# Cross-attention mask of a decoder layer: four slices of 32 keys against a small identity, in place of a 63-row product in two passes

## The chip, the cores and the metric

One core of one Trainium2 chip runs the whole kernel. The metric is the device time of one execution in microseconds (us); a median over several runs is compared. Line numbers (L290) are those of the kernel before.

## The reference, cut to what matters

The program is one pre-norm decoder layer over 32 batches of 128 rows by 128 features, all in f32: self-attention with 16 heads of 8, then cross-attention with 16 heads of 64, then a mixture of 8 experts (one per row, picked by an argmax) with a shared expert. The change is in the cross-attention:

```python
def xattn(q, k, v, wq, wk, wv, wo):
    qh, kh = rope(q @ wq.T), rope(k @ wk.T)            # 16 heads of 64
    scores = einsum('bhqd,bhkd->bhqk', qh, kh) * 64 ** -0.5
    i, j = arange(128)[:, None], arange(128)[None, :]
    scores = where((j <= i) & (j >= i - 32), scores, -1e30)
    out = einsum('bhqk,bhkd->bhqd', softmax(scores), v @ wv.T)
    return out @ wo.T
```

So a query sees its own key and the 32 before it; every other score is -1e30. The mask is the same for all heads and batches.

## The kernel before, in words

Each engine has its own instruction stream, written out by hand, and the streams meet on semaphores. All five run over 42 periods; in period s each stage works on a batch of its own (`batch(f, s - k)`): the self-attention of batch s-4 stands between the cross-attention scores of batch s-5, the cross-attention's transposes and products of batch s-6 and the router and shared expert of batch s-7. From period 32 on, tiles of rows sorted by expert (`x_tr`, `x_up`, `x_hT`, `x_dn`) are mixed in; a second set of such tiles follows the last period. PSUM is one tensor `P` of 8 banks of 128 x 512 f32; the table `BANK` names a bank for each use, and `take` makes TensorE wait until the engine that last read that bank is done.

The order on TensorE around the change, in one period: `b_st` (L215, L219: the self-attention scores of batch s-4, keys on the partitions, and the row maxima folded in by bf16 matmuls with 12 rows in each of the four row tiles), `d_pv` (L318), `d_s` (L290, L298), `b_pv` (L230), `f_pos` (L365 to L369), `d_wo` (L329), `b_oT` (L238).

`d_s(b)` makes the cross-attention scores of batch b in four banks, one for each row tile r of the array (partitions 32r to 32r+31); a bank holds four heads as 4 x 128 columns. It first writes the mask, then adds the products of queries and keys onto it (L298, 32 f32 matmuls, which the trace counts as 64). The mask before is a product of 63 rows: `rows` says which queries a row stands for, `cols` has 0 or -1e30 for the 128 keys. 63 rows do not fit into 32 partitions, so there are two passes h, each with four bf16 matmuls (one for each r) of 32 rows against 512 columns (the 128 of `cols`, repeated for the four heads). Both tables are cut from the constant `cb`, which ScalarE's queue loads once at the start.

Who touches this work: the first matmul of `d_s` waits for its four banks (ds0 is bank 3, which `b_st` used as st2 and ScalarE reads in `b_ps(b, 2)`, L753). L298 waits for `p_k` and `p_q`, GpSimd's additions L946 and L951. After the last L298, `t_ds` releases VectorE's maxima `d_max` (L559), these ScalarE's exponentials `d_exp` (L789). `f_pos` on TensorE waits for GpSimd's `f_acc` (L966). `b_oT` waits for ScalarE's copy L760, which stands behind the first `d_exp` in ScalarE's stream.

Of the kernel before, what the change touches and what calls it, by code (L numbers as in the profile page):

```python
# [6 lines left out]
BF16 = mybir.dt.bfloat16  # L7
U32 = mybir.dt.uint32
U16 = mybir.dt.uint16
# [43 lines left out]
def build(nc, A):  # L53
    ctx = ExitStack()
    with ctx:
        def sb(name, shape, dt=F32):
            return ctx.enter_context(nc.sbuf_tensor(name, shape, dt))
# [8 lines left out]


        c1 = sb("c1", [128, 646])
        cb = sb("cb", [128, 1296], U16)
        c2 = sb("c2", [128, C2])  # L70
        tab = sb("tab", [128, 4, 2, 128])
        ones = sb("ones", [128, 128], BF16)
# [59 lines left out]
        identb, upper = cb[:, 0:128].bitcast(BF16), cb[:, 128:256].bitcast(BF16)  # L132
        sel = cb[:, 256:768].bitcast(BF16).rearrange("p (j k) -> p j k", j=4)
        ecap = cb[:, 768:784].bitcast(BF16).rearrange("p (c e) -> p c e", c=2)
        rows, cols = (cb[:, 784 + 256 * k:1040 + 256 * k].bitcast(BF16).rearrange("p (h n) -> p h n", h=2) for k in range(2))
        woutT, bo, fill, tri = c2[:, 0:128], c2[:, 128:256], c2[:, 256:256 + ROW], c2[:, 528:592]
        tri = tri.rearrange("p (a b) -> p a b", a=8)
        rtT, iota, ids = c2[:, 592:600], c2[:, 600:608], c2[:, 608:640].bitcast(U32)
# [3 lines left out]
        def v3(ap):  # L142
            return ap.rearrange("p (a n) -> p a n", n=128)
# [26 lines left out]
        def _(pe):  # L170
            held = {}

            def take(slot, *until):
                for sem, value in held.get(BANK[slot], ()):
                    pe.wait_ge(sem, value)
                held[BANK[slot]] = until
                return P[:, BANK[slot], :]
# [107 lines left out]

            def d_s(b):
                p = [take(f"ds{r}", (S["s_ex"][r], b + 1)) for r in range(4)]
                for h in range(2):
                    for r in range(4):
                        pe.matmul(v3(p[r]), rows[32 * r:32 * r + 32, h, :],  # L290
                                  cols[32 * r:32 * r + 32, h, :].rearrange("p (a k) -> p a k", a=1).to_broadcast([32, 4, 128]),
                                  start=(h == 0), stop=False, skip_group_check=True)
                pe.wait_ge(S["p_k"], b + 1)
                pe.wait_ge(S["p_q"], b + 1)
                for c in range(4):
                    for e in range(2):
                        for r in range(4):
                            t = pe.matmul(p[r][:, c * 128:c * 128 + 128], rq[b % 2][32 * r:32 * r + 32, e, c, :],  # L298
                                          rk[b % 2][32 * r:32 * r + 32, e, c, :], start=False, stop=(c == 3 and e == 1),
                                          skip_group_check=True)  # L300
                t.then_inc(S["t_ds"], 1)
# [103 lines left out]
            for s in range(PERIODS):  # L405
# [34 lines left out]
                batch(d_pv, s - 6, 0)  # L440
                batch(d_pv, s - 6, 1)
                batch(d_s, s - 5)
                batch(b_pv, s - 4)
                batch(f_pos, s - 7)
# [739 lines left out]
```

## Time and profile before

| | |
|---|---|
| Median of 3 runs | 804.68 us (804.55 to 804.92) |
| The profiled execution's own time | 806.58 us |
| Its span, first to last instruction | 804.8 us |
| TensorE busy | 94% of the span |
| VectorE, ScalarE, GpSimd busy | 66%, 67%, 67% |
| Mean granted TensorE clock | 0.984 |
| L290, the mask: 256 matmuls | 19.5 us busy in all, mean 379 ns |
| L219, the nearest relative: 512 matmuls, 12 rows, 128 columns, bf16 | 13.2 us busy in all, mean 217 ns |

A matmul's duration runs from its start until its result is in PSUM, and matmuls overlap, so the pace of TensorE is read from start to start and not from durations. In the timeline a row is a group of equal instructions that follow each other: its start, its length (first start to last end) and its count. An f32 matmul of the program stands in the trace as two.

### The profile page before, as it was taken

How to read it: one execution, taken by the hardware profiler on the slowest of the kernel's cores; microseconds unless marked ns; L12 is line 12 of the kernel's file. 1: busy time of each engine (PE TensorE's matmuls, PEld its weight loads, DVE VectorE, ACT ScalarE, POOL GpSimd, SP SyncE). 2: the span in 40 equal slices, each digit the busy share in tenths (PEclk: the TensorE clock that was granted, in tenths of full speed). 3: DMA queues.
4: the chain of work that ended last, by engine and by line, in shares of the span. 5: the costliest groups of instructions: out<-in, count | busy, mean ns of one | idle time of the engine just before them, and what ended most of it. 6: DMA issues, size and time to landing. Idle time of an engine off the chain costs nothing. (4 is left out here: it accounts for less than half of the span.)

```text
span 804.8 us, 27623 instructions
## 1 busy us (share of the span) xinstructions
PE 760.4 (94%) x9852; PEld 623.1 (77%) x9852; DVE 531.7 (66%) x1350; ACT 537.5 (67%) x1900; POOL 536.5 (67%) x864
## 2 busy tenths in 40 slices
PE   4889999999999999999999999999899999998893
PEld 2668888888888888888888888888678777876552
DVE  3566776777777767777777767777866685555652
ACT  2367777777777777777777777777577566656451
POOL 4366777777777777777777777777575755565543
PEclk9799999999999999999999999999999999999997
DMA  6031233323222222221111122223150202333230
GB/s 234 8 119 64 91 91 91 91 83 90 89 91 71 70 72 71 70 68 59 60 58 58 67 71 71 71 71 127 68 151 3 81 24 83 103 102 105 69 101 12
DMA packets 56789, 64.01 MB, mean 80 GB/s; under 512 B 4015, under 2 KB 52917, under 8 KB 56657
## 3 DMA queue, kind: packets, MB, share of 16 engines
q1 hardware_dynamic: 52928, 54.06, 21.0%
q0 software_dynamic: 3008, 6.57, 2.4%
q8 instruction: 83, 1.36, 0.7%
q10 hardware_dynamic: 720, 1.62, 0.5%
q14 instruction: 50, 0.40, 0.2%
HBM read 17.79 MB, written 45.35 MB: 78 GB/s over the span
## 5 line engine op out<-in xcount | busy, mean ns | idle before, releaser
L789 ACT ACTIVATE PX<-P,mx 128x128 f32<-128x128 f32 x512 | 183.5, 409 | 67.5 <-DVE mx L559 67.5
L559 DVE TENSOR_REDUCE mx<-P 128x4 f32<-128x512 f32 x128 | 83.1, 674 | 155.4 <-PE P L298 155.4
L956 POOL TENSOR_TENSOR PX<-PX,mx 128x512 f32<-128x512 f32 x128 | 133.2, 1042 | 14.0 <-DVE mx L564 13.9
L789 ACT ACTIVATION_READ_ACCUMULATOR PX<-P,mx 128x1 f32 x512 | 127.2, 248 | 0.0
L951 POOL TENSOR_TENSOR rq<-rq,tq 128x1024 f32<-128x1024 f32 x32 | 75.6, 2363 | 60.5 <-DVE rq L523 60.5
L753 ACT ACTIVATE PS<-P 128x512 f32<-128x512 f32 x128 | 70.6, 607 | 24.9 <-PE P L219 24.9
L498 DVE TENSOR_REDUCE nmf<-P 128x4 f32<-128x512 f32 x128 | 81.3, 679 | 7.0 <-PE P L198 4.2
L798 ACT ACTIVATE PT<-P 128x512 f32<-128x512 f32 x128 | 76.5, 597 | 8.2 <-PE P L307 5.7
L307 PE MATMUL P<-c,PX 128*128 128x128 f32 x512 | 79.3, 278 | 0.0
L307 PEld LDWEIGHTS P<-c,PX 128*128 128x128 f32 x512 | 57.4, 142 | 24.1 <-issue 22.7
L946 POOL TENSOR_TENSOR rk<-rk,tk 128x1024 f32<-128x1024 f32 x32 | 75.5, 2359 | 0.0
L273 PEld LDWEIGHTS P<-cxT,wk 128*128 128x128 f32 x512 | 64.4, 197 | 8.9 <-issue 8.9
L273 PE MATMUL P<-cxT,wk 128*128 128x128 f32 x512 | 69.7, 280 | 0.0
L298 PEld LDWEIGHTS P<-rk,rq 32*128 32x128 f32 x2048 | 64.2, 187 | 6.4 <-issue 2.0
L263 PE MATMUL P<-wvT,cxT 128*128 128x512 f32 x128 | 68.4, 617 | 0.0
L298 PE MATMUL P<-rk,rq 32*128 32x128 f32 x2048 | 65.2, 271 | 1.1 <-issue 1.0
L902 POOL TENSOR_SCALAR st<-st 128x1 f32<-128x1 f32 x96 | 22.2, 231 | 66.0 <-DVE st L467 61.2
L329 PE MATMUL P<-woT,oX 128*128 128x128 f32 x512 | 65.0, 280 | 0.6 <-ACT oX L805 0.6
L318 PE MATMUL P<-PT,V 128*64 128x128 f32 x1024 | 63.0, 276 | 0.0
L283 PE MATMUL P<-cT,wq 128*128 128x128 f32 x512 | 62.5, 275 | 0.3 <-ACT cT L773 0.3
L989 POOL DMA_INDIRECT out<-yst,xrow x46 | 45.2, 983 | 25.5 <-issue 14.9
L329 PEld LDWEIGHTS P<-woT,oX 128*128 128x128 f32 x512 | 59.6, 192 | 0.8 <-issue 0.8
(140 smaller groups left out, 1767.5 us busy)
## 6 DMA issues: line engine op xcount, KB each, us to landing
z_xs<-c SPq DMA_DIRECT2D x34, 1088.0 KB, 5.2
xrow<-z_xs SPq DMA_DIRECT2D x46, 136.0 KB, 3.3
ew<-in_ew SPq DMA_DIRECT2D x9, 384.0 KB, 3.8
x<-in_x SPq DMA_DIRECT2D x32, 64.0 KB, 1.8
cxT<-in_ctxT SPq DMA_DIRECT2D x31, 64.0 KB
out<-yst,xrow POOLq DMA_INDIRECT x46
wk<-in_wk SPq DMA_DIRECT2D x1, 512.0 KB, 4.5
wvT<-in_wvT SPq DMA_DIRECT2D x1, 512.0 KB, 7.1
```

The lines of the kernel that those rows point to most:

```text
L273: t = pe.matmul(p[:, c * 128:c * 128 + 128], wk[:, e, c, :], cxT[b % 4][:, :], start=True, stop=True)
L298: t = pe.matmul(p[r][:, c * 128:c * 128 + 128], rq[b % 2][32 * r:32 * r + 32, e, c, :], rk[b % 2][32 * r:32 * r + 32, e, c, :], start=Fals ...
L307: t = pe.transpose(p[:, c * 128:c * 128 + 128], PX[(4 * b + r) % 6][:, c, :], ident[:, :])
L329: t = pe.matmul(p[:, 0:128], oX[2 * (b % 2) + k][:, q, :], woT[:, 4 * k + q, :], start=(k == 0 and q == 0), stop=(k == 1 and q == 3))
L498: dve.tensor_reduce(nmf[b % 2][:, 0, r, :], v3(bank(f"s{r}")), AX.X, ALU.max, negate=True).then_inc(S["v_bm"][r], 1)
L559: dve.tensor_reduce(mx[b % 3][:, 0, r, :], v3(bank(f"ds{r}")), AX.X, ALU.max, negate=True).then_inc(S["v_dm"][r], 1)
L753: act.activation(PS[(4 * b + r) % 6][:, :, :].rearrange("p h q -> p (h q)"), bank(f"st{r}"), ACT.Exp, scale=S_SELF).then_inc(S["s_ps"][r], 1)
L789: t = act.activation(PX[(4 * b + r) % 6][:, c, :], p[:, c * 128:c * 128 + 128], ACT.Exp, bias=m[:, 0, r, c:c + 1], scale=1.0, accum_out=m[ ...
L798: act.activation(PT[(4 * b + r) % 6][:, :, :].rearrange("p h q -> p (h q)"), bank(f"dt{r}"), ACT.Copy).then_inc(S["s_pt"][r], 1)
L946: pool.tensor_tensor(rk[b % 2][:, :, :, :], rk[b % 2][:, :, :, :], tk[:, :, :, :], ALU.add).then_inc(S["p_k"], 1)
L951: pool.tensor_tensor(rq[b % 2][:, :, :, :], rq[b % 2][:, :, :, :], tq[:, :, :, :], ALU.add).then_inc(S["p_q"], 1)
L956: pool.tensor_tensor(X[:, :, :], X[:, :, :], mx[b % 3][:, 2, r, :].rearrange("p (h a) -> p h a", a=1).to_broadcast([128, 4, 128]), ALU.mul ...
```

## The change

`d_s` writes the mask in four slices w of 32 keys. The stationary operand is `far[:, w, :]`: partition k holds, for all 128 queries, the mask's value for key 32w + k. The moving operand is a 32 x 32 identity `eye`, repeated for the four heads, and the product lands in columns 32w to 32w+31 of each head. There are 16 matmuls of 32 rows against 128 columns for a batch in place of 8 against 512 columns. The first slice has the start flag in place of the first pass. `cb` grows from 1296 to 1328 columns of 2 bytes.

```diff
-        cb = sb("cb", [128, 1296], U16)
+        cb = sb("cb", [128, 1328], U16)
...
-        rows, cols = (cb[:, 784 + 256 * k:1040 + 256 * k].bitcast(BF16).rearrange("p (h n) -> p h n", h=2) for k in range(2))
+        far, eye = cb[:, 784:1296].bitcast(BF16).rearrange("p (w q) -> p w q", w=4), cb[:, 1296:1328].bitcast(BF16)
...
             def d_s(b):
                 p = [take(f"ds{r}", (S["s_ex"][r], b + 1)) for r in range(4)]
-                for h in range(2):
+                for w in range(4):
                     for r in range(4):
-                        pe.matmul(v3(p[r]), rows[32 * r:32 * r + 32, h, :],
-                                  cols[32 * r:32 * r + 32, h, :].rearrange("p (a k) -> p a k", a=1).to_broadcast([32, 4, 128]),
-                                  start=(h == 0), stop=False, skip_group_check=True)
+                        pe.matmul(v3(p[r])[:, :, 32 * w:32 * w + 32], far[32 * r:32 * r + 32, w, :],
+                                  eye[32 * r:32 * r + 32, :].rearrange("p (a k) -> p a k", a=1).to_broadcast([32, 4, 32]),
+                                  start=(w == 0), stop=False, skip_group_check=True)
...
-    near = lambda q: (j <= q) & (j >= q - 32)
-    sets = [row[r::58] for r in range(58)] + [row[26 * r:26 * r + 26] for r in range(5)]
-    rows, cols = np.zeros((2, 64, 128), f)
-    for k, q in enumerate(sets):
-        rows[k, q], cols[k] = 1, np.where(near(q[:, None]).any(axis=0), f(0), f(-1e30))
-    four = lambda a: np.tile(a.reshape(2, 32, 128).transpose(1, 0, 2).reshape(32, 256), (4, 1))
+    seen = (row[None, :] >= row[:, None]) & (row[None, :] <= row[:, None] + 32)
+    far = np.tile(np.where(seen, f(0), f(-1e30)).reshape(4, 32, 128).transpose(1, 0, 2).reshape(32, 512), (4, 1))
...
-                           four(rows), four(cols)], axis=1).astype(f)
+                           far, np.tile(np.eye(32), (4, 1))], axis=1).astype(f)
```

## Rows read from the trace of the kernel before

**Rows 1.** The page: busy time of each engine.
```profile
PE 760.4 (94%) x9852; PEld 623.1 (77%) x9852; DVE 531.7 (66%) x1350; ACT 537.5 (67%) x1900; POOL 536.5 (67%) x864
```

**Rows 2.** The waits of all engines: who waited for whom, us in total, times, longest.
```profile
DVE mx L559 <- PE P L298: 155.4, 32, 7.4
...
PEld P L290 <- ACT PS L753: 6.8, 30, 1.8
...
PEld P L365 <- issue: 6.0, 30, 0.2
```

**Rows 3.** Timeline of TensorE, one steady period and the next L290: start, length, engine, line, count.
```profile
414.55 0.40 PE L219 MATMUL P<-nmT,cb 12*128 12x128 bf16 x16
414.88 1.97 PE L318 MATMUL P<-PT,V 128*64 128x128 f32 x32
416.78 0.61 PE L290 MATMUL P<-cb 32*128 32x512 bf16 x8
417.22 1.95 PE L298 MATMUL P<-rk,rq 32*128 32x128 f32 x64
419.10 1.08 PE L230 MATMUL P<-PS,vpad 128*32 128x128 f32 x32
420.12 0.18 PE L365 MATMUL P<-cb,ones 128*128 128x8 bf16 x1
...
420.23 2.03 PE L329 MATMUL P<-woT,oX 128*128 128x128 f32 x16
...
437.58 0.61 PE L290 MATMUL P<-cb 32*128 32x512 bf16 x8
```

**Rows 4.** Timelines of ScalarE, VectorE and GpSimd in the same period.
```profile
414.99 1.57 ACT L753 ACTIVATE PS<-P 128x512 f32<-128x512 f32 x3 [0.74 <-PE P L219]
...
421.37 0.61 ACT L760 ACTIVATE oT<-P 128x512 f32<-128x512 f32 x1
...
419.25 0.69 DVE L559 TENSOR_REDUCE mx<-P 128x4 f32<-128x512 f32 x1 [4.68 <-PE P L298]
...
413.66 2.37 POOL L951 TENSOR_TENSOR rq<-rq,tq 128x1024 f32<-128x1024 f32 x1 [1.64 <-DVE rq L523]
...
419.65 0.21 POOL L966 TENSOR_TENSOR acc<-acc,OH 128x8 bf16<-128x8 bf16 x1
```

**Rows 5.** Timeline of TensorE in two narrow windows: the first four and first twelve of L219.
```profile
414.55 0.24 PE L219 MATMUL P<-nmT,cb 12*128 12x128 bf16 x4
...
414.55 0.35 PE L219 MATMUL P<-nmT,cb 12*128 12x128 bf16 x12
```

**Rows 6.** The same: the second four of L290, the first eight of L298.
```profile
417.01 0.38 PE L290 MATMUL P<-cb 32*128 32x512 bf16 x4
417.22 0.39 PE L298 MATMUL P<-rk,rq 32*128 32x128 f32 x8
```

**Rows 7.** L290's loads (ns, min/median/max); starts of two groups of f32 matmuls.
```profile
L290 PEld LDWEIGHTS P<-cb x256: 90/92/94, 42.0 to 720.0; 32*128 32x128 bf16 x128
...
413.55 0.50 PE L215 MATMUL P<-qT,KM 32*128 32x128 f32 x7
...
420.23 0.47 PE L329 MATMUL P<-woT,oX 128*128 128x128 f32 x2
```

**Rows 8.** Timeline of the weight loads around L238.
```profile
421.43 0.64 PEld L329 LDWEIGHTS P<-woT,oX 128*128 128x128 f32 x5
422.09 0.42 PEld L238 LDWEIGHTS P<-c,oT 128*128 128x128 f32 x4
```

**Rows 9.** Timeline of TensorE in a late period, with expert tiles mixed in.
```profile
669.66 1.44 PE L298 MATMUL P<-rk,rq 32*128 32x128 f32 x29
671.37 1.38 PE L298 MATMUL P<-rk,rq 32*128 32x128 f32 x35 [0.27 <-issue]
672.69 1.08 PE L230 MATMUL P<-PS,vpad 128*32 128x128 f32 x32
```

**Rows 10.** A stretch by windows: busy us of each engine, clock, DMA share, GB/s.
```profile
574.00:578.00 4.00, 4.00 (x17) 2.00 (x16) 3.03 (x9) 2.33 (x11) 3.40 (x6) 0.57 0.02 4
```

## The prediction

> **What bounds the kernel now.** I read the page's busy times first. TensorE is busy 94% of the span and the next engine 67% [rows 1], at a mean granted clock of 0.984. Then I read the waits, to see whether the other engines pace TensorE or it paces them. The longest wait of all is VectorE's, for the last L298 of `d_s`: 155.4 us over 32 batches [rows 2], and the timeline shows one of these, 4.68 us in a period of 20.8 [rows 3, 4]. The weight loads of L290 do show a wait for ScalarE, 6.8 us in all or 0.2 us a batch, and those of L365 an equal 0.2 us for "issue" [rows 2]. I take both for the same thing: L318 and L230 use only part of the array's columns, and after such a group the next kind of tile starts some 0.2 us after the last matmul, whoever it waits for. ScalarE's three exponentials were over at 414.99 + 1.57 = 416.56, 0.22 us before L290 starts at 416.78 [rows 3, 4]. The third view, TensorE's timeline, gives what the mask costs: L290 starts at 416.78 and L298 at 417.22, so 0.44 us of every batch, made of 0.23 us from the first four matmuls to the second four, and 0.21 us from these to L298 [rows 3, 6]. The four row tiles work side by side: four matmuls of 512 columns take the time of one. What the change is worth is this stretch, if TensorE's time there is the kernel's time.
>
> **Removed:** the two sets of four matmuls with 512 columns, 0.44 us from L290's start to L298's.
>
> **Added:** four sets of four with 128 columns, bf16, 32 rows. The trace has one operation that is nearly this, L219: bf16, four row tiles, 128 columns, four sets. Its first four have a length of 0.24 us, the first twelve 0.35 and all sixteen 0.40 us [rows 3, 5], so three more sets take 0.16 us, some 0.055 us each. The first set of L290 took about 0.015 us longer than the second (0.23 to 0.21), since nothing hides its load; I keep this. So L298 would start 4 x 0.055 + 0.015 = 0.235 us after L290, not 0.44.
>
> **What comes back at once.** The f32 loads of L298 now have 0.215 us of mask matmuls to hide under, afterwards only 0.055 us. What an uncovered f32 load costs is in two groups. L215's first four start with nothing ahead of them: the seventh matmul starts 0.50 - 0.27 = 0.23 us after the first, so the second set comes 0.21 us after the first where sets otherwise follow every 0.11; 0.10 us is lost. L329's first has only the 0.025 us of a small matmul ahead: its second starts 0.47 - 0.275 = 0.195 us after it, 0.08 us lost [rows 7]. Between these, with 0.055 us of cover, about 0.05 us is lost (estimate, 0.104 less the cover). In the kernel before L298's second set starts 0.11 us after the first [rows 6], nothing lost.
>
> The sum for a batch, to L298's second set: before 0.44 + 0.11 = 0.555; after 0.235 + 0.11 + 0.05 = 0.395; gain 0.16 us. Bounds: without the lost load time 0.21; with the whole 0.10 of L215, 0.11. I take 0.16, since the cover lies between the two measured cases.
>
> **What I can't see in this trace** is a matmul whose output and moving operand go in pieces of 32 columns. Nearest are L219, whose pieces of 128 cost nothing visible (0.055 us is 128 columns at the pace of L290's 512 in 0.215), and f32 matmuls of the same 128 columns, which take 0.11 us a set [rows 6]. I take 0.055, because L219 has the same engine mode, type and count, and keep 0.11 as the other end.
>
> **Does the gain reach the end?** From `t_ds` on, VectorE, ScalarE and GpSimd follow L298, so they come earlier with it. Only what was started before L290 and is waited for after it can hold it back. (1) L298 waits for GpSimd's L951, over at 413.66 + 2.37 = 416.03, over a microsecond early [rows 3, 4]. (2) L230 waits for ScalarE, whose queue is then empty until the maxima come. (3) L365 waits for GpSimd's L966, over at 419.86; L365 starts at 420.12 [rows 3, 4]. Where TensorE really waits for another engine, at L238, the load comes 0.11 us after ScalarE's copy ends (421.98 and 422.09) [rows 4, 8], so L365 has 0.26 - 0.11, about 0.15 us to give. (4) Behind it L238 is itself held by that copy: five loads of L329 with a length of 0.64 start every 0.11 us, the next was due at 421.99 and comes at 422.09, of which some 0.05 us shows in the matmuls [rows 8]. That copy follows `t_ds`, so it comes earlier in full, and L365 may be 0.05 us late without cost. Together 0.20 us of gain can pass, and 0.16 does. `d_s` is on TensorE's path in all 32 batches, the last too, since the maxima of batch 31 wait for it. 32 x 0.16 = 5.1 us.
>
> **The rest of the edit.** `cb` grows by 64 bytes a partition, 8 KB, once, in a start where it is first used for the transpose after the first self-attention scores: nothing; uncovered it would be under 0.1 us. TensorE gets 8 more matmuls and 8 more loads a batch; their supply is a rival below.
>
> The profiled execution took 806.58 us, 1.9 above the median of 804.68; the terms are differences inside it, and I take them off the median: 804.7 - 5.1 = 799.6.
>
> **Rivals.** (B) *Each set waits for its own loads.* A bf16 load takes 0.092 us [rows 7]. If sets of 128 columns follow at that pace, L298 starts at 4 x 0.092 + 0.015 = 0.383, the f32 load loses 0.01, and the gain is 0.05 us a batch, 1.6 us: 803.1. L219 speaks against it: its loads are as long and its sets come every 0.055 us. The Trainium skill (TensorE: Matmul & The Clock Gate, Back-to-back issue gap) states a rule of this kind against the change: in streams of load and matmul, 81 ns for 128 columns and 131 ns for 512. Taken for our sets that is 4 x 81 = 324 against 2 x 131 = 262 ns, a loss of 2.0 us. The trace disagrees at both ends, 55 and 215 to 227 ns, which is why B gets little.
>
> (C) *The pieces of 32 columns halve the pace.* Sets at 0.11 us: L298 starts at 0.455, no load time is lost, 0.013 us a batch worse, 805.1. Break-even is a set of 0.107 us. For it: nothing in the trace has such pieces. Against it: the columns that flow are the same in number as L219's.
>
> (D) *Slower: the instructions do not come fast enough.* In late periods L298 breaks off: 29 matmuls, then a gap marked "issue", then 35, and 3.03 us until L230 where a steady period needs 1.88 (417.22 to 419.10): 1.15 us lost, in two or three breaks of about 0.5 [rows 3, 9]. No other engine is named, so it is the supply of TensorE's own stream, in its densest part, and the change puts 16 more instructions right ahead of it. Thirteen more such breaks of 0.5 us turn the sum to slower by over 0.2%; one in each of the 26 steady batches would give 804.7 - 5.1 + 13 = 812.6. Against it: L215, L219 and L318 bring 80 matmuls, each with its load, in 3.2 us of a steady period (413.55 to 416.78), and L298 64 in 1.9, without a break [rows 3, 7].
>
> A term of either sign: the clock fell to half after TensorE waited around 570 us (0.57 over 4 us [rows 10]). The periods before it will end some 4 us earlier, so such a dip may vanish or one may be added, up to 1.7 us.
>
> **How the numbers follow.** My case has 0.74, B 0.08, C 0.10, D 0.06, and 0.02 is left for a new clock dip or stall that eats all. The case itself reaches from 32 x 0.11 = 3.5 us (801.2) to 32 x 0.21 = 6.7 (798.0), less where L365 caps it; with the dip 1 us further down, 797.0. The upper end is pulled to 803.2 to take B in; left out are C, D and the tails. 0.2% of this kernel, 1.6 us, is about what a measurement can tell from no change. Faster by more: 0.74 and a third of B, 0.77. Within: the rest of B and C, 0.15. Slower: D and the remainder, 0.08.
>
> **What would show it.** In the changed profile L290 should have 512 matmuls of about 215 ns; from its start to L298's about 0.235 us; L298's first four should last some 0.05 us longer than the 270 of the rest; steady periods should be 20.64 in place of 20.80 us; VectorE's wait for L298 should shrink by about 0.16 x 32 = 5 us; L365 should start 0.11 to 0.15 us after GpSimd's L966. C would show as sets 0.11 us apart, B as sets 0.09 apart, D as rows of L298 with "issue" in steady periods. I am wrong if L298 starts 0.235 us after L290 and the periods still last 20.8: then a wait that I counted as loose holds them.

## The result, and the profile after

The changed kernel's median is 798.47 us (796.53 to 800.97, 11 runs), that of the kernel before 802.34 (800.20 to 804.92, 11 runs). The ratio is 0.9949, with a 95% interval of 0.993 to 0.9968: 4.1 us faster, 2.6 to 5.6. The forecast was 0.9936 of the median then known, 5.1 us. Three of the 11 runs of the kernel before are the ones it was known by ahead of the prediction, and they are its three slowest; the median of the other eight is 801.69, and against these the changed kernel is 3.2 us faster. The profiled execution took 799.48 us, its span is 797.7.

The page of the changed kernel, busy time, answers to [rows 1]; VectorE's wait for the last L298, in all and in one steady period, to [rows 2] and [rows 4]:

```profile
PE 754.8 (95%) x10108; PEld 622.4 (78%) x10108; DVE 531.7 (67%) x1350; ACT 537.8 (67%) x1900; POOL 535.2 (67%) x864
...
DVE mx L559 <- PE P L298: 146.9, 32, 5.8
...
417.58 0.69 DVE L559 TENSOR_REDUCE mx<-P 128x4 f32<-128x512 f32 x1 [4.53 <-PE P L298]
```

TensorE has 256 more matmuls and 5.6 us less busy time; the other engines' busy time changes by 1.3 us at most. VectorE's wait shrank by 8.5 us in all, where 5 were forecast: the steady periods give the 5 (4.68 to 4.53 us each), the rest fits the late breaks described below, though no run separates it. The timeline of TensorE in a steady period and the start of the next one answers to [rows 3]:

```profile
415.26 0.40 PE L290 MATMUL P<-cb 32*128 32x128 bf16 x16
415.49 2.01 PE L298 MATMUL P<-rk,rq 32*128 32x128 f32 x64
417.43 1.08 PE L230 MATMUL P<-PS,vpad 128*32 128x128 f32 x32
418.48 0.17 PE L365 MATMUL P<-cb,ones 128*128 128x8 bf16 x1
...
422.36 1.04 PE L263 MATMUL P<-wvT,cxT 128*128 128x512 f32 x2
423.41 0.46 PE L251 MATMUL P<-c,cnT 128*128 128x128 f32 x2
...
435.91 0.40 PE L290 MATMUL P<-cb 32*128 32x128 bf16 x16
```

Read it against [rows 3]. L290 to L298 is 0.234 us, where it was 0.442 (the expectations below say 0.237 and 0.446, a few ns too much). L298 to L230 is 1.94 us, where it was 1.88: 0.056 us came back, the f32 loads that lost their cover. The two together give 0.152 us a batch. The period, L290 to L290, is 20.65 us, where it was 20.80 (the median of 20 such periods is 20.81). The first two are the same in every steady batch to 3 ns; the period is so in 17 of 20 periods before and in 19 of 20 after, and the others are 0.1 to 0.3 us longer.

The duration of L290 alone would mislead. Its mean fell from 379 to 217 ns, but a matmul of 128 columns shows 0.21 us in a stream in which four of them start every 0.055 us.

**GpSimd and L365.** The timeline of GpSimd in the same period answers to the last line of [rows 4]:

```profile
415.81 2.36 POOL L946 TENSOR_TENSOR rk<-rk,tk 128x1024 f32<-128x1024 f32 x1
418.13 0.20 POOL L966 TENSOR_TENSOR acc<-acc,OH 128x8 bf16<-128x8 bf16 x1
```

L966 ends at 418.33 and L365 starts 0.15 us later. It was 0.26 before, and 0.15 is the least that a waiting TensorE showed. So L365 is held now. With `f_acc` early (after_acc below) it comes 0.03 us sooner after L230.

**What the steady periods leave over.** 32 x 0.152 is 4.9 us, but the profiled execution is 7.1 us shorter than that of before (806.58 to 799.48). The steady periods do not explain the rest. The late breaks inside L298 [rows 9] were 3 us and more in the first trace and absent in this one, while a half-speed stretch at the start lasted 13.7 us in place of 10.2. The same window of both traces, before and after:

```profile
18.00:38.00 20.00, 14.52 (x139) 11.64 (x140) 9.98 (x19) 5.98 (x14) 6.98 (x17) 0.74 0.04 11
```

```profile
18.00:38.00 20.00, 14.53 (x126) 10.71 (x127) 8.43 (x18) 5.98 (x14) 6.13 (x13) 0.66 0.03 7
```

The granted clock is 0.74 in one and 0.66 in the other, and the first L290 comes at 42.0 and 43.6 us. So two whole traces can't be subtracted from each other; the steady periods can. The longer table `cb` is not the reason: in the trace of the changed kernel its load ends at 6.6 us, and TensorE first reads it at 20.2.

That the medians show less than 4.9 us may lie here. The mean granted clock is 0.9825 on average over the 42 runs of the kernel before that were measured with the experiments, 0.9813 over the 11 of the changed kernel and 0.9803 over the 11 of after_acc. If TensorE's time counted everywhere, that would cost 1.0 to 1.8 us (an estimate: 0.0012 and 0.0022 of 800 us). No run shows whether the change moves the clock or chance does.

### The profile page after: what moved, and what is told of

The parts are those of the page before. It is cut to its first block and busy times, and to the rows that moved or that the text cites. A ratio compares the mean times of both kernels' runs of the same rounds, so it can differ in the third digit from the quotient of the medians.

```text
span 797.7 us, 28135 instructions
## 1 busy us (share of the span) xinstructions
PE 754.8 (95%) x10108; PEld 622.4 (78%) x10108; DVE 531.7 (67%) x1350; ACT 537.8 (67%) x1900; POOL 535.2 (67%) x864
## 5 line engine op out<-in xcount | busy, mean ns | idle before, releaser
L263 PE MATMUL P<-wvT,cxT 128*128 128x512 f32 x128 | 68.8, 621 | 0.0
L298 PE MATMUL P<-rk,rq 32*128 32x128 f32 x2048 | 65.2, 276 | 0.0
L318 PE MATMUL P<-PT,V 128*64 128x128 f32 x1024 | 63.0, 276 | 0.0
L298 PEld LDWEIGHTS P<-rk,rq 32*128 32x128 f32 x2048 | 60.7, 189 | 0.0
L283 PEld LDWEIGHTS P<-cT,wq 128*128 128x128 f32 x512 | 59.7, 192 | 0.6 <-issue 0.5
```

The source lines that it names most:

```text
L283: t = pe.matmul(p[:, c * 128:c * 128 + 128], wq[:, e, c, :], cT[b % 2][:, :], start=True, stop=True)
```

## The experiments

Each kernel was profiled, and some were timed beside the kernel before. The table holds what the traces show of batch 5 and on: the period is the median of 20 steady ones, from L298 to L298. Line numbers of the experiments are shifted by a few lines where their edit adds or takes lines (the scores are L293 in the two without a mask, L299 in fine16 and double, L300 in cn3 and at3). A kernel without a ratio was run once, and its numbers are those of that one trace. Times in us.

| kernel | L290 to L298 | L298 to L230 | period | ratio to before, 95% interval |
|---|---|---|---|---|
| before | 0.442 | 1.88 | 20.81 | 1 |
| before, again | 0.442 | 1.88 | 20.79 | |
| changed | 0.234 | 1.94 | 20.65 | 0.9949 (0.993 to 0.9968) |
| changed, again | 0.233 | 1.94 | 20.64 | |
| nomask | none | 2.00 | 20.56 | 0.9923 (0.9898 to 0.9947) |
| nomask_acc | none | 2.00 | 20.45 | 0.9875 (0.9853 to 0.9897) |
| heads | 0.234 | 1.94 | 20.65 | |
| fine16 | 0.243 | 2.01 | 20.69 (20.67 to 20.96) | 0.998 (0.9955 to 1.0005) |
| double | 0.457 | 1.94 | 20.86 | 1.0012 (0.9988 to 1.0036) |
| onepass_acc | 0.226 | 1.88 | 20.58 | |
| cn3 | 0.234 | 1.94 | 20.64 | |
| at3 | 0.234 | 1.94 | 20.87 | |
| after_acc | 0.233 | 1.94 | 20.64 | 0.9952 (0.9937 to 0.9967) |
| acc_swap | 0.234 | 1.94 | 21.22 | 1.0199 (1.0181 to 1.0217) |

**Both kernels again.** No edit.

> The kernel before, profiled once more, to see which differences between the first two traces belong to the change. If the breaks inside L298 in the late periods belong to the longer mask, they return at the same places, about 0.07, 1.1, 1.4 and 0.9 us in the last four batches. If they are chance of one execution, they are gone or lie elsewhere. Steady periods must be 20.80 us, L290 to L298 0.446 us. The half-speed stretch at the start was 10.2 us long before and 13.7 after; if that is chance, it may differ here too.

> The changed kernel, profiled once more. Steady periods 20.65 us, L290 to L298 0.237 us. By the theory that breaks inside L298 and the length of the half-speed stretches are chance, either may appear here; by the theory that the change removed the breaks, there are none.

The steady numbers returned. The breaks appeared in both. TensorE's timeline late in the second trace of the kernel before, and late in that of the changed kernel:

```profile
667.20 1.61 PE L298 MATMUL P<-rk,rq 32*128 32x128 f32 x32
669.07 1.22 PE L298 MATMUL P<-rk,rq 32*128 32x128 f32 x32 [0.25 <-issue]
```

```profile
666.90 0.98 PE L298 MATMUL P<-rk,rq 32*128 32x128 f32 x18
668.09 0.47 PE L298 MATMUL P<-rk,rq 32*128 32x128 f32 x3 [0.21 <-issue]
668.84 1.62 PE L298 MATMUL P<-rk,rq 32*128 32x128 f32 x43 [0.28 <-issue]
670.39 1.08 PE L230 MATMUL P<-PS,vpad 128*32 128x128 f32 x32
```

So neither mask makes or removes them. The four traces of this group (both kernels again, nomask and nomask_acc), taken on one chip, all have them. The first trace of the kernel before has them and the first of the changed kernel has not. Of the eight later traces, on two other chips, seven have none inside these late groups of scores and acc_swap has one of 0.7 us. The kernel before was slower there as well: its median was 807.47 us in that group, 801.77 and 802.33 in the two others. That points at the chip or the placement, but no run here separates the two, and why the stream of instructions breaks stays open.

**No mask at all.** It leaves out the mask of the cross-attention.

```diff
-                for w in range(4):
-                    for r in range(4):
-                        pe.matmul(v3(p[r])[:, :, 32 * w:32 * w + 32], far[32 * r:32 * r + 32, w, :],
-                                  eye[32 * r:32 * r + 32, :].rearrange("p (a k) -> p a k", a=1).to_broadcast([32, 4, 32]),
-                                  start=(w == 0), stop=False, skip_group_check=True)
...
-                                          rk[b % 2][32 * r:32 * r + 32, e, c, :], start=False, stop=(c == 3 and e == 1),
+                                          rk[b % 2][32 * r:32 * r + 32, e, c, :], start=(c == 0 and e == 0), stop=(c == 3 and e == 1),
```

> Leaves the mask of the cross-attention out: no L290 at all, the first scores carry the start flag. TensorE alone would gain, against the changed kernel, 0.237 + 0.11 + 0.056 less the 0.21 us of an uncovered first f32 set, so 0.19 us a batch. Theory 1 (GpSimd's addition for f_pos, behind two long additions, holds L365, and TensorE has only about 0.02 us more to give at L238): steady periods stop at about 20.63 us, L365 starts no earlier against L318 than in the changed kernel, and the whole gains under 1 us on it. Theory 2 (TensorE's time alone counts): periods of 20.46 us, 6 us less than the changed kernel.

**No mask, and GpSimd's f_acc early.**

```diff
-                batch(r_ka, s - 4)
                 batch(f_acc, s - 7)
+                batch(r_ka, s - 4)
```

> The same without the mask, and GpSimd does f_acc ahead of the addition for rk (L946) in place of behind it. Theory 1: the hold at L365 is gone, steady periods fall to about 20.46 us. Theory 2: as without the move. If something else holds the periods (ScalarE's copy in front of L238, the exponentials), they stay near 20.63 in both.

TensorE's timelines, first without the move and then with it:

```profile
411.60 2.07 PE L293 MATMUL P<-rk,rq 32*128 32x128 f32 x64
413.60 1.08 PE L230 MATMUL P<-PS,vpad 128*32 128x128 f32 x32
414.85 0.17 PE L360 MATMUL P<-cb,ones 128*128 128x8 bf16 x1 [0.17 <-POOL acc L961]
...
418.72 1.06 PE L263 MATMUL P<-wvT,cxT 128*128 128x512 f32 x2
419.61 0.42 PE L251 MATMUL P<-c,cnT 128*128 128x128 f32 x2
...
432.18 2.07 PE L293 MATMUL P<-rk,rq 32*128 32x128 f32 x64
```

```profile
413.85 2.07 PE L293 MATMUL P<-rk,rq 32*128 32x128 f32 x64
415.85 1.08 PE L230 MATMUL P<-PS,vpad 128*32 128x128 f32 x32
416.86 0.18 PE L360 MATMUL P<-cb,ones 128*128 128x8 bf16 x1
...
434.31 1.96 PE L293 MATMUL P<-rk,rq 32*128 32x128 f32 x60
```

The hold is real: without the move, f_pos (L360 here, L365 in the changed kernel) comes 1.25 us after L230 in this period (1.23 in the median) and the profile now names GpSimd; with it, 1.01. Without the move f_pos starts as long after L318 as in the changed kernel, to 0.03 us. With the move the period is 20.45 us, as theory 1 said. But without it the period is 20.56 and not the 20.63 expected: 0.09 of the 0.19 us passed although L365 did not move. Something behind L365 gives way. Between L263 and L251 there are 1.05 us in the changed kernel (422.36 to 423.41) and 0.89 here (418.72 to 419.61). This led to the next two runs.

**Where TensorE's time counts.** Two transposes more, in either of two places; the result is the same.

```diff
             def b_cn(b):
...
+                pe.transpose(p[:, 0:128], cn[b % 2][:, :], ident[:, :])
+                pe.transpose(p[:, 0:128], cn[b % 2][:, :], ident[:, :])
                 pe.transpose(p[:, 0:128], cn[b % 2][:, :], ident[:, :]).then_inc(S["t_cn"], 1)
```

> The changed kernel with the transpose L244 of b_cn done three times in place of once, so 0.22 us more of TensorE's time a batch, between the scores and L251. Theory 1: from the last score to L251 ScalarE's chain (maxima, exponentials, copy L766 of what L244 made) sets the time, and TensorE has 0.19 us to spare there (L263 to L251 1.05 us, where the other L263 takes 0.86): the period rises by some 0.03 us to 20.68. Theory 2, TensorE's time counts wherever it is spent: 20.87 us.

```diff
             def a_tr(b):
...
+                pe.transpose(p[:, 0:128], arow[b % 2][:, :], ident[:, :])
+                pe.transpose(p[:, 0:128], arow[b % 2][:, :], ident[:, :])
                 pe.transpose(p[:, 0:128], arow[b % 2][:, :], ident[:, :]).then_inc(S["t_a"], 1)
```

> The changed kernel with the transpose L184 of a_tr done three times in place of once: the same 0.22 us a batch, between L251 and the next L318. Theory 1 and 2 both say it counts in full here: 20.87 us. If it doesn't, TensorE is held by another engine in this part too, and the reading of the chain is wrong.

Ahead of L251 the 0.22 us cost nothing that shows (period 20.64, as in after_acc on the same chip), behind it they cost 0.22 (20.87). Timelines of TensorE: cn3 (L265 is the L263 of before, L253 the L251), then at3 (L292 is the mask):

```profile
423.06 1.02 PE L265 MATMUL P<-wvT,cxT 128*128 128x512 f32 x2
423.92 0.42 PE L253 MATMUL P<-c,cnT 128*128 128x128 f32 x2
```

```profile
417.38 0.40 PE L292 MATMUL P<-cb 32*128 32x128 bf16 x16
...
438.24 0.40 PE L292 MATMUL P<-cb 32*128 32x128 bf16 x16
```

L265 to L253 shrank to 0.86 us: the two transposes took up the wait. In the kernel before, L263 to L251 is 1.05 us too, so the wait was there already. Who holds L251 is in ScalarE's timeline and the weight loads of the changed kernel:

```profile
418.30 0.37 ACT L789 ACTIVATE PX<-P,mx 128x128 f32<-128x128 f32 x1 [1.79 <-DVE mx L559]
...
422.57 0.44 ACT L789 ACTIVATE PX<-P,mx 128x128 f32<-128x128 f32 x1
422.82 0.28 ACT L789 ACTIVATION_READ_ACCUMULATOR PX<-P,mx 128x1 f32 x1
422.91 0.35 ACT L766 ACTIVATE cnT<-P 128x128 f32<-128x128 f32 x1
```

```profile
423.38 0.30 PEld L251 LDWEIGHTS P<-c,cnT 128*128 128x128 f32 x2 [0.80 <-issue]
```

The maxima start once the scores are there (417.58, shown above) and the first exponential follows at 418.30. From then on ScalarE has no pause: it copies `cnT` only when the exponentials of `d_exp` 1, 0 and 2 are through, and the copy ends at 423.26, 0.12 us before the load of L251. From L298's second set to L251 it was 7.75 us in the kernel before and 7.75 in the changed one. In this third of the period a chain of VectorE and ScalarE sets the time, and it starts with the scores.

**Pieces of 32 columns.** Same count and same loads, but the output in one piece; most of the mask is left out.

```diff
-                        pe.matmul(v3(p[r])[:, :, 32 * w:32 * w + 32], far[32 * r:32 * r + 32, w, :],
-                                  eye[32 * r:32 * r + 32, :].rearrange("p (a k) -> p a k", a=1).to_broadcast([32, 4, 32]),
+                        pe.matmul(p[r][:, 128 * w:128 * w + 128], far[32 * r:32 * r + 32, w, :],
+                                  identb[32 * r:32 * r + 32, :],
```

> Sixteen mask matmuls as in the changed kernel, with the same stationary operands, but each writes one head's 128 columns in one piece from the 128 columns of an identity, in place of four pieces of 32. Most of the mask is left out by this. If pieces of 32 columns cost nothing, L290 to L298 stays 0.237 us and the period 20.65. If they cost something, it is shorter than 0.237.

The mask stage and the period are the same, so pieces of 32 cost nothing here.

**Slices of 16 keys.**

```diff
-                for w in range(4):
+                for w in range(8):
                     for r in range(4):
-                        pe.matmul(v3(p[r])[:, :, 32 * w:32 * w + 32], far[32 * r:32 * r + 32, w, :],
-                                  eye[32 * r:32 * r + 32, :].rearrange("p (a k) -> p a k", a=1).to_broadcast([32, 4, 32]),
+                        pe.matmul(v3(p[r])[:, :, 16 * w:16 * w + 16], far[32 * r:32 * r + 32, w // 2, :],
+                                  eye[32 * r:32 * r + 32, 16 * (w % 2):16 * (w % 2) + 16].rearrange(
+                                      "p (a k) -> p a k", a=1).to_broadcast([32, 4, 16]),
```

> The same mask in eight slices of 16 keys: 32 matmuls of 64 columns, in pieces of 16. If the columns that flow set the pace, L290 to L298 stays near 0.24 us, or 0.26. If the number of instructions does (sixteen matmuls and loads took 7 ns each in the changed kernel), it is 8 x 0.055 + 0.015 = 0.455 us, the period 20.87 and the time 5 to 7 us above the changed kernel.

TensorE's timeline, of a steady period and of an earlier one with a break in the mask:

```profile
416.39 0.41 PE L290 MATMUL P<-cb 32*128 32x64 bf16 x32
416.63 2.08 PE L299 MATMUL P<-rk,rq 32*128 32x128 f32 x64
418.63 1.08 PE L230 MATMUL P<-PS,vpad 128*32 128x128 f32 x32
...
270.80 0.58 PE L290 MATMUL P<-cb 32*128 32x64 bf16 x32
271.32 2.07 PE L299 MATMUL P<-rk,rq 32*128 32x128 f32 x64
```

In most batches thirty-two matmuls with their loads take the time of sixteen, 0.243 us, so columns set the pace down to 64 of them, in pieces of 16. Neither the number of instructions nor a bf16 load of 0.09 us does. What it loses is behind: the second set of scores comes 0.19 us after the first, where it is 0.11 in the kernel before and 0.165 in the changed one, because only 0.03 us of a set is left ahead of the first f32 load. That and the 0.009 us of the mask stage give the 0.04 us by which the median period is above the changed kernel's.

But in five of the 28 batches from the fifth on the mask stage takes 0.26 to 0.52 us, in the second period shown because the last of the 32 matmuls comes late, and other groups start up to 0.23 us late in more periods. The mean of the steady periods is 20.75 us, 0.09 above the changed kernel's 20.66, and over 32 batches that is 2.9 us; the ratios, 0.998 against 0.9949, differ by 2.5, with intervals that overlap. The changed kernel's mask stage shows no such break in a steady batch, and neither does that of double, which has as many instructions with twice the columns. So the number of instructions does count once each brings only 64 columns. The profile names no engine for these gaps; that the instructions come too slowly is the likely cause and not shown.

**The mask twice.**

```diff
-                for w in range(4):
+                for u in range(8):
+                    w = u % 4
...
-                                  start=(w == 0), stop=False, skip_group_check=True)
+                                  start=(u == 0), stop=False, skip_group_check=True)
```

> The changed kernel with the four slices written twice, so the mask is -2e30. TensorE's time in front of the scores counts in full by every theory that has d_s on the path: L290 to L298 0.237 + 4 x 0.055 = 0.457 us, period 20.87 us, all back and a little more than the kernel before. If other work hid it, the period would stay below that.

As expected: 0.22 us more ahead of the scores are 0.21 us more of period (against heads, on the same chip). Time there counts one for one. The whole kernel is back at the one before (1.0012), with a mask stage of nearly the same length.

**One pass of the mask before,** with f_acc early; part of the mask is left out.

```diff
-                for h in range(2):
+                for h in range(1):
```

> The kernel before with the first of its two passes alone (part of the mask is left out) and GpSimd's f_acc ahead of L946, so that nothing holds L365. Four matmuls of 512 columns take as many columns as the sixteen of the changed kernel, but leave 0.21 us of cover for the f32 loads of L298. If cover is what costs 0.056 us in the changed kernel: L290 to L298 0.231, L298 to L230 1.883 and not 1.939, period 20.59 us. If the 0.056 belongs to something else (many small instructions), L298 to L230 stays 1.94.

```profile
414.23 0.39 PE L290 MATMUL P<-cb 32*128 32x512 bf16 x4
414.46 1.95 PE L298 MATMUL P<-rk,rq 32*128 32x128 f32 x64
416.34 1.08 PE L230 MATMUL P<-PS,vpad 128*32 128x128 f32 x32
```

As many columns as the changed kernel's mask, but L298 to L230 is back at 1.88. So the 0.056 us are the cover of the f32 loads, and the price rises with what is missing. From the first set of scores to the second it is 0.056 us with 0.055 us of matmul ahead, 0.083 with 0.03 (fine16) and 0.104 with none (nomask). From the first score to L230 it is 0.056, 0.12 and 0.115: in the last two the four row tiles run further out of step, and L230 starts 0.20 us after the last of them.

**The changed kernel with f_acc early, and with L198 ahead of L251 as well.**

> The changed kernel, with GpSimd's f_acc ahead of the addition L946. In the changed kernel L365 waits for f_acc and comes 0.03 us late, but L251 waits for ScalarE all the same, so nothing is gained in steady periods: 20.65 us, within 0.2% of the changed kernel. If the hold at L365 counts, 20.62.

```diff
-                batch(b_x1, s - 5)
                 batch(b_s, s - 4)
+                batch(b_x1, s - 5)
```

> The same, and TensorE does b_s (L198) ahead of b_x1 (L251), so that it works while ScalarE's copy L766 is under way. If the 0.19 us wait in front of L251 is what keeps TensorE from its own pace: periods of 20.46 us, 5 us less than the changed kernel. Against it: VectorE does its part of b_x1 ahead of the maxima of b_s and would wait about 0.85 us longer for L251, which delays the normalisation behind L256; if that is held then, the periods are longer than 20.65.

The first gains nothing that can be told: 20.64 us, and 0.9952 against 0.9949. The second tries to fill the wait in front of L251 and is 2% slower than the kernel before. TensorE's timeline of acc_swap:

```profile
414.39 1.14 PE L198 MATMUL P<-KM,qT 32*128 32x512 f32 x8
415.46 0.49 PE L251 MATMUL P<-c,cnT 128*128 128x128 f32 x2
418.83 0.30 PE L256 MATMUL P<-c,lnr 128*128 128x128 f32 x1 [0.58 <-ACT lnr L708]
```

TensorE no longer waits in front of L251, but L251 comes 1.1 us later, and after VectorE's statistics, GpSimd and ScalarE's normalisation L256 waits 0.58 us. No version tried with a full mask beats the changed kernel.

## Why the prediction was right, and where it was not

**The mask stage.** Forecast 0.235 us from L290 to L298, measured 0.234. L219 was the right relative, and its pace held for pieces of 32 (heads). The rivals B and C fall with this: sets came every 0.055 us, not every 0.09 or 0.11. The rule of the Trainium skill cited with B (TensorE: Matmul & The Clock Gate, Back-to-back issue gap: 81 ns for 128 columns) does not hold for this mask either, since by it the change would have lost time.

**The cover of the f32 loads.** Forecast 0.05 us lost, measured 0.056, shown to be cover by onepass_acc. The estimate behind it, 0.104 less the cover, fits all three cases to 7 ns: 0.049 for the changed kernel, 0.076 against 0.083 in fine16, 0.104 against 0.104 in nomask.

**The sum.** Forecast 0.16 us a batch and 20.64 us a period, measured 0.152 and 20.65. Over 32 batches that is 4.9 us; the runs show 4.1, with 4.9 inside their interval. That the whole came out 0.8 us lower than the batches add up to is not explained; the granted clock is a candidate (see above).

**L365.** Forecast to be 0.11 to 0.15 us behind GpSimd's L966; it is 0.15 and held, so it comes 0.12 us earlier and not 0.15. That this costs nothing was right.

**What could pass in all: wrong in its size.** The prediction said "Together 0.20 us of gain can pass", 0.15 at L365 and 0.05 at L238. Nomask passed 0.23 against the kernel before on the same chip (20.79 to 20.56), with L365 held, and 0.34 with `f_acc` early (20.45). The step that failed is (4): it stopped at L238 and took TensorE as the bound from there on. L251 waits another 0.19 us a batch for ScalarE (cn3). It did not matter for 0.16. For a longer saving it would have made the forecast too low where L365 is held.

**The first reading, that TensorE paces the others, was half right.** From L251 to the last score TensorE sets the time (shown at the two places where at3 and double add to it); from there to L251 VectorE and ScalarE do. VectorE's wait for L298 shows only that it idles in the first of the two. The gain arrived because the mask stands in the part that is TensorE's.

**Rival D** did not come. The changed kernel has 16 more instructions ahead of L298 and breaks off there only where the kernel before does too. Its mechanism is not empty, though: fine16, with 32 more instructions than the changed kernel, does show gaps in steady periods. One sum of D is slightly off: thirteen more breaks of 0.5 us give 806.1, 0.17% above 804.7, so it takes fourteen to pass 0.2%. The dips of the clock moved, as allowed for; no run tells that the change moved them.

## What to carry to other kernels

The price of a mask or bias that goes into PSUM by matmul was here the columns that flow, not the matmuls: four narrow slices against a small identity took half the time of two wide passes, with half the columns, and pieces of 32 columns cost nothing. There is an end to this: slices of 16 keys (64 columns) kept the pace in most batches but brought gaps in others, and their mean period was longer. Keep the last small matmul ahead of an f32 group long enough to cover its first load: 0.21 us of matmul hid it whole, 0.055 us half of it. A busy share of 94% doesn't make an engine the bound everywhere: look in each part of the period for a short wait on another engine, since in front of it TensorE's time costs nothing and a saving there gains nothing.

## What the runs showed of the hardware that was not expected

Four bf16 matmuls of 64 columns in four row tiles, each with its own load of 128 columns, follow each other every 0.028 us in most batches (fine16), half of the 0.055 us of 128 columns, although one load shows a length of 0.09 us. An f32 group that begins on idle row tiles loses 0.104 us by its first loads (nomask). Breaks of about 0.5 us inside a dense group of matmuls, marked "issue", came at nearly the same place in every trace of one group of runs and in almost none of the others; their cause is open.
